# A wait two tiles older and four PSUM slots instead of two in the first layer norm's transposes

## The reference

```python
x = L0_attn_x                                   # [16, 2048, 1024] float32
x = x + _layernorm(attn(_layernorm(x)))         # 16 heads of 64, causal, w_q/w_k/w_v/w_u
x = x + _layernorm(ffn(_layernorm(x)))          # recurrence over the 16 batches, then a tanh layer

def _layernorm(x, eps=1e-5):
    m = jnp.mean(x, axis=-1, keepdims=True); v = jnp.var(x, axis=-1, keepdims=True)
    return (x - m) / jnp.sqrt(v + eps)
```

## Time and profile before

| | us |
|---|---|
| median of 3 runs | 7089.46 (7085.5 to 7363.37) |
| the profiled execution | 7080.41 |
| its span on the slowest core (core 2) | 7078.5 |
| spans of the 8 cores | 7043.2 to 7078.5 |
| mean granted clock of the 8 cores | 0.752 to 0.760 |
| busy: TensorE matmul / VectorE / ScalarE / GpSimd | 67% / 31% / 21% / 6% |

### The profile page before, as it was taken

One profiled execution on the slowest core, in us unless ns is written; L12 is line 12 of the kernel. 1 busy time (PEld: TensorE's weight loads), 2 busy tenths in 40 slices (PEclk: granted clock), 3 DMA queues, 4 the chain that ended last, 5 costly groups with the idle time before them and its releaser, 6 DMA issues.

```text
span 7078.5 us, 84637 instructions; the slowest of 8 cores (7043.2 to 7078.5 us)
## 1 busy us (share of the span) xinstructions
PE 4724.2 (67%) x31769; PEld 3003.1 (42%) x31972; DVE 2206.7 (31%) x3874; ACT 1485.9 (21%) x2697; POOL 420.8 (6%) x367
## 2 busy tenths in 40 slices
PE   4876868777686876868677686877333129999222
PEld 2544444444444444444444444444111118887110
DVE  2232322323233232322324232232222333333333
ACT  1213141221313212141221313122000002222222
POOL 3010010101001010010101001010000000000000
PEclk9877868788686877868787786877555559999666
DMA  4011010101101010110101101010222220000222
GB/s 101 1 57 34 24 57 1 57 1 57 51 7 57 1 57 24 34 57 1 57 1 57 43 15 57 1 57 10 66 71 69 93 82 13 13 13 14 92 94 92
DMA packets 95066, 299.11 MB, mean 42 GB/s; under 512 B 14800, under 2 KB 14800, under 8 KB 94672
## 3 DMA queue, kind: packets, MB, share of 16 engines
q1 hardware_dynamic: 90000, 285.30, 12.3%
q0 software_dynamic: 4672, 8.39, 0.8%
HBM read 268.49 MB, written 33.55 MB: 43 GB/s over the span
## 4 chain that ended last, share of the span: by engine, by line
PE 59%; DVE 13%; ACT 11%; issue 7%; DMA 7%; POOL 2%; SPq 1%; DVEq 0%; ACTq 0%; POOLq 0%
PE PA L386 13%; PE PB L403 12%; PE PA L267 7%; PE PB L701 5%; PE PB L464 5%; PE PB L690 4%; ACT ex L500 3%; PE PB L429 3%; ACT lnf L277 3%; PE PA L480 3%; PE PA L597 2%; DVE of L532 1%; PE PB L771 1%; PE PA L544 1%; DMA va<-alns 1%
## 5 line engine op out<-in xcount | busy, mean ns | idle before, releaser
L500 ACT ACTIVATE ex<-PA 128x1024 bf16<-128x1024 f32 (+15 forms) x1024 | 625.1, 624 | 2702.3 <-PE PA L490 2656.5
L386 PE MATMUL PA<-lnf,wk_sb 128*128 128x512 bf16 x4000 | 923.2, 392 | 47.4 <-ACT of L277 42.6
L403 PE MATMUL PB<-wv_sb,lnf 128*128 128x512 bf16 x4016 | 882.5, 379 | 4.2
L386 PEld LDWEIGHTS PA<-lnf,wk_sb 128*128 128x128 bf16 x4096 | 410.6, 101 | 558.4 <-issue 130.5
L464 PE MATMUL PB<-ex,va 128*65 128x256 bf16 (+15 forms) x4096 | 482.3, 242 | 204.0 <-ACT ex L500 124.7
L403 PEld LDWEIGHTS PB<-wv_sb,lnf 128*128 128x128 bf16 x4096 | 400.8, 98 | 483.3
L267 PE MATMUL PA<-identf,lt 128*128 128x128 f32 x1152 | 273.1, 415 | 466.3 <-POOL lt L260 245.6
L393 DVE CAST kf<-PA 128x512 bf16<-128x512 f32 x512 | 354.1, 692 | 702.4 <-PE PA L386 702.4
L480 PE MATMUL PA<-qf,kf 128*128 128x256 bf16 (+15 forms) x4096 | 515.0, 256 | 22.1 <-DVE qf L440 22.1
L411 DVE CAST va<-PB 128x1024 bf16<-128x1024 f32 x256 | 314.1, 1227 | 578.5 <-PE PB L403 578.5
L267 PEld LDWEIGHTS PA<-identf,lt 128*128 128x128 f32 x1152 | 220.7, 218 | 520.1 <-issue 520.1
(11 more groups left out here) (99 smaller groups left out, 4937.6 us busy)
## 6 DMA issues: line engine op xcount, KB each, us to landing
xt<-xg SPq DMA_DIRECT2D x128, 512.0 KB, 3.8
xt<-xm SPq DMA_DIRECT2D x96, 512.0 KB, 4.5
ex<-xg SPq DMA_DIRECT2D x64, 512.0 KB, 4.5
of<-xg SPq DMA_DIRECT2D x64, 512.0 KB, 3.9
va<-alns SPq DMA_DIRECT2D x64, 256.0 KB, 4.8
va<-ln2s SPq DMA_DIRECT2D x32, 512.0 KB, 3.9
y<-lt SPq DMA_DIRECT2D x32, 512.0 KB, 3.0
alns<-ex SPq DMA_DIRECT2D x32, 256.0 KB, 2.0
```

Source lines behind the costliest of these rows:

```text
L386: P.op("tensor", lambda t, dmc=dmc, hp=hp, g4=g4, po=po: t.matmul(PA[:, po:po + 512], wk[:, 1024 * dmc + 128 * hp: 1024 * dmc + 128 * (hp ...
L403: P.op("tensor", lambda t, dmc=dmc, kt=kt, hf=hf, po=po: t.matmul(PB[:, po + 512 * hf: po + 512 * (hf + 1)], lnf[:, 2048 * dmc + 128 * kt: ...
L500: P.op("scalar", lambda s, vs=vs, slot=slot, idx=idx: s.activation(sub3(ex, 1024 * (idx % 2) + vs, [256, 4], [1, 256 - vs]), sub3(PA, slot ...
```

## The change

TensorE's wait for evacuations in `emit_ln_tile_bf` asks for a count that is lower by two: for tile k, the evacuation of tile k-4. The transposes rotate over four destinations instead of two: the two halves of `PA` and the two halves of `PB`. The evacuation reads from where they went. At the start of each batch TensorE also waits for `ve_norm`. What ScalarE, GpSimd, VectorE and SyncE wait for in this stage is as before, and no instruction is added or removed besides that wait.

```diff
     P.wait("tensor", "gp_lnapply")
-    P.wait("tensor", "ve_Tevac")
-    po = 1024 * par2
+    P.wait("tensor", "ve_Tevac", max(P.v("ve_Tevac") - 2, 0))
+    pslot = k % 4
+    pbuf = PA if pslot < 2 else B["PB"]
+    po = 1024 * (pslot % 2)
     for ch in range(8):
-        P.op("tensor", lambda t, ch=ch, po=po, lt=lt: t.transpose(
-            PA[:, po + 128 * ch: po + 128 * (ch + 1)],
+        P.op("tensor", lambda t, ch=ch, po=po, lt=lt, pbuf=pbuf: t.transpose(
+            pbuf[:, po + 128 * ch: po + 128 * (ch + 1)],
             lt[:, 128 * ch:128 * (ch + 1)], B["identf"][:]),
             inc="te_T" if ch == 7 else None)
@@ evac()
         P.wait("scalar", "te_T")
         P.op("scalar",
-             lambda sc, po=po, dst_col=dst_col, dst_fm=dst_fm, stride=stride:
+             lambda sc, po=po, dst_col=dst_col, dst_fm=dst_fm, stride=stride,
+             pbuf=pbuf:
              sc.copy(
                  sub3(dst_fm, dst_col, [stride, 8], [1, 128]),
-                 sub3(PA, po, [128, 8], [1, 128])),
+                 sub3(pbuf, po, [128, 8], [1, 128])),
              inc="ve_Tevac")
@@ emit_attention(), at the start of each batch
         P.wait("tensor", "ve_al")
+        P.wait("tensor", "ve_norm")
```

## The result

The changed kernel takes 0.9831 of the time before (95% interval 0.981 to 0.9853, ten executions of each): 1.7% faster, about 120 us. The executions that the ratio compares took 6961.6 to 6989.4 us, the three of before 7085.5 to 7096.1. In some executions of either kernel the chip holds one die or both at a lower clock for a while, which costs up to some per cent; the ratios leave them out. The profiled execution took 6971.25 us, its slowest core (core 4) 6969.4.

What follows compares the result with a forecast made beforehand. TensorE and ScalarE were taken to alternate at 3.18 us a tile; a 5.20 us loop for two tiles saves 6.85 a stage, plus 0.88 for clock: 16 x 7.73 = 124 us, predicting 6965 us, range 6900 to 7010.

Steps and rivals of the forecast that it cites:

- The sum: Whole kernel: 16 stages at 7.73 us each save 124 us, ratio 0.9825, giving 6965 us on the median.
- within 2%: Class for the whole kernel's time, taken as no measurable change: chance 0.64, against 0.32 faster and 0.04 slower.
- The wait: TensorE's 238 waits for the evacuation, 298.2 us, would go near zero, with waits for GpSimd's L260 in their place.
- The loop of 5.20: New loop over evacuation, Ln, normalization and transposes: 5.20 us for two tiles, 2.60 a tile against 3.18.
- The stage: First transposes to K projection: ends at 50.75 us without further clock rises, against a mean of 57.60, 6.85 less.
- The clock: TensorE's clock in transposes: about one further short rise a stage, giving 7.73 us; full clock throughout gives 12.1.
- the rival of a clock that stays up: Transposes: three to six clock rises a stage gain 9.5 to 12.1 us each stage, 6895 to 6935 in all; 28%.
- my 0.88: Transpose loop: us that one clock rise shortens it by, added once to the 6.85 a stage.
- The loads: Loop over four slots takes 7.74 us against 10.40 for four tiles, so loads stay hidden; rival that they bind, 9%.
- `ve_norm`, `PB`, the K projection's start: Added wait at batch start and evacuation from `PB` cost nothing; last transposes to K projection stays 4.74 us.
- the change does nothing: Rival: an unseen wait on the same place, candidate ScalarE's for transposes of k-1; price 0, 7089 us; 4%.
- The rival that the projections' clock falls: K and V projections: denser transposes lengthen their low-clock stretch, up to net 18 us a batch, 290 in all, 7380; 4%.

Runs made afterwards that it cites:

- the doubling: GpSimd's normalization of each tile done twice, on the changed kernel and on the kernel before: 7177.8 us and 7183.2 us.
- `xm` edit: Kernel before with evacuation waiting for its own tile's transposes, plus both `xm` tiles loaded over all four slots: 6782.9 and 6792.5 us, about 0.960.
- `te_own`: Evacuation waits for its own tile's transposes instead of the next tile's; on the kernel before, ratio 0.9725.

## Why the prediction was right, and where it failed

**What failed is the class, not the time.** The sum gave a ratio of 0.9825, and 0.9831 was measured. But the prediction took about 2% for "what a measurement of this kernel can tell from no change" and so put 0.64 on within 2%, a forecast of a gain of 1.75% that counted as no change. No row stood behind these 2%, and two of the three times of the kernel before, 7085.5 and 7089.5, lay 0.06% apart. The comparison told the gain from none, 0.9831 with an interval of 0.2% on either side. A sum whose every term stands in a row and whose sign no rival but one at 4% disputes was a forecast of faster, and had to be given as one. The step that failed is the one from the sum to the chances: it held 2% to be what can't be told from no change, and the runs showed 0.2%.

**The wait.** Right: the waits for the evacuation went from 238 to none that is really one, and those for L260 took their place.

**The loop of 5.20.** Right: 5.21 from 991.76 to 996.97, term by term (2.03, 0.91, 0.82, 1.45), and shown to hold GpSimd's operation by the doubling, 6.57 against 6.56 worked out. Over the 16 stages, two tiles of one parity are 5.21 apart in the median where the first of them and the tile between ran at the low clock (73 pairs); with the fast ones the mean is 4.99. That the two parities would start 1.87 and 3.3 apart holds only at the stage's start: later they stood 2.40 and 2.81 apart in this stage (991.76, 994.16, 996.97), and the fast tiles 5 to 7 lie where the distance changed. That the fast clock shifts one loop against the other is argued from this, not tested. It changes nothing in the sum.

**The stage.** 49.87 predicted, 49.50 measured on core 2. Tile 17 came at 46.05 where 46.01 was worked out, but with two errors that cancel: tile 15's normalization was earlier (34.77 for 36.82), and its follower's way of 9.19 took 11.28, because the load took 5.8 us from issue to statistics instead of 3.69.

**The clock.** The sign was right, the count and the size were not. The windows read 0.57 to 0.70 in the 16 stages on core 2, against my 0.50 to 0.60; in the fourth, tiles 5, 6 and 7 at 1.07, 1.06, 1.06 are one such stretch, and the loop in it is 984.62 - 980.28 = 4.34, against the bound of 4.32. A single rise had shown as 0.53; the excess over 0.50 is now two to seven times that. TensorE's busy time says the same: 30.89 us in the mean stage against 34.84 at 0.50 makes 3.95 / 0.88, about four and a half tiles a stage at the full clock where before it was half a tile. So what the rival of a clock that stays up asked for, three to six rises a stage, did come in the mean, and by its price the stage would have gained 9.5 to 12.1 us; it gained 8.1. Yet the whole effect is 50.75 - 49.50 = 1.25 us, less than two of my 0.88.

The term was mis-sized because two loops run side by side, and a short stretch of fast clock speeds one tile in each or in only one, where I let each rise take its whole 0.88 off the end. In the mean of the 16 stages tile 15 starts at 36.64 instead of 38.27, 1.63 earlier; of that, tile 17's way from tile 15's normalization takes back 0.52 (9.71 instead of 9.19, its load being slower), and the way to the K projection gives 0.13. So the forecast of 0.88 and the measured 1.25 lie close by luck: I forecast about a quarter of the fast tiles and three times the worth of each.

The rule of the Trainium skill that transposes don't bring the full clock (the Trainium skill, TensorE: Matmul & The Clock Gate, Part 4: PE-mode transpose) is contradicted again: no stage of the changed kernel on core 2 reads below 0.57.

**The loads.** Right that they stay hidden up to tile 15: of the 176 tiles 5 to 15 on core 2, Ln stood behind VectorE in 9 and else behind the evacuation. The median landing rose to 4.5 us, a first sign of what binds the next version, and the 2.66 us to spare covered it.

**`ve_norm`, `PB`, the K projection's start.** Free, as costed; the way from tile 17's transposes to the K projection is 4.59 (4.74 predicted).

**What it overlooked.** The prediction named ScalarE's wait for the tile after only as a candidate for "the change does nothing", and wrote of it that the loop contains it. It does; but it is the root, and the 12 to 13 us a stage from one corrected value were there to be worked out from the same rows.

**The rival that the projections' clock falls** did show itself, on two cores. In the profiled execution cores 4 and 5 had their first projections at 0.81 and core 2 at 1.00; windows of core 4, then core 2:

```profile
150.00:240.00 90.00, 89.38 (x337) 37.26 (x343) 27.65 (x33) 0.00 (x0) 0.00 (x0) 0.81 0.00 1
```

```profile
150.00:240.00 90.00, 89.53 (x409) 40.79 (x417) 33.49 (x37) 0.00 (x0) 0.00 (x0) 1.00 0.00 1
```

Core 4's batches 1 and 2 took 267.0 and 256.4 us from the K projection to the next stage, core 2's 247.8 and 245.4. That is 30.2 of the 36.9 us by which core 4's span is longer than core 2's. It was the whole effect of this rival here, far from its 290 us. The traces of the kernel before, of the four destinations alone and of both doubled kernels show it on no core; those with the wait one evacuation younger and with the evacuation waiting for its own tile show it again on cores 4 and 5, in the first one or two batches. Those of the changed kernel without the wait for `ve_norm` and of the timed `xm` edit, with stages as dense or denser, do not. Whether the denser stages cause it is open.

## What to carry to other kernels

When a wait's value is taken from a counter at the moment of emission, and the emission is delayed behind other work, the wait asks for too much; look at what releases an operation in the trace (here the transposes of the tile after) before adding buffers, since the corrected value beat the extra buffers and made them useless. When such a turn is broken, write the next loop out with its period in tiles: the old one had one tile, the new one two, the corrected one three (where the loop of the loads, over four tiles, binds first), and the period decides as much as the sum. And size a forecast's class by the measurement's own spread, not by a round 2%.

## What the runs showed of the hardware that I had not expected

- Float32 transposes alone raise TensorE's clock from 0.50 to 1.00 and keep it there for several tiles when they follow each other closely: 0.57 to 0.70 over a stage of the changed kernel, and 0.76 to 0.82 in the first three stages of the version with the `xm` edit, with eight transposes at 1.06 us instead of 1.94.
- A load of 512 KB took longer as the loads came closer, 3.8 us in the median at one tile in 3.18 us (kernel before), 4.5 at about 2.5 (changed kernel) and 4.6 at about 2.2 (kernel before with `te_own`), with the DMA engines 0.4 to 0.6 busy over a stage.
